# One adaptive-layer and mixture-of-experts kernel: silu ahead of a weight split in tiles 2 to 4, VectorE's tile word read one tile sooner, the fourth expert's weights ahead of the first copies

## The reference

```python
base = jnp.einsum('bsi,oi->bso', x, W_base)
h = jnp.einsum('bsi,ji->bsj', x, Wt)
z = jnp.einsum('bsj,brj->bsr', h, Ab)                    # A[adapter_idx]
l = jnp.einsum('bsr,bor->bso', z, Bb)                    # B_w[adapter_idx]
y = base + jnp.einsum('bso,po->bsp', l, Wp) * sc[:, None, None]
...
probs = jax.nn.softmax(jnp.dot(y, gate_w.T), axis=-1)
topk_w, topk_idx = jax.lax.top_k(probs, TOP_K)           # TOP_K = 2, weights normalised
g = jnp.einsum('th,eih->tei', y, w_gate)                 # INTER = 352
u = jnp.einsum('th,eih->tei', y, w_up)
h = jax.nn.silu(g) * u
expert_out = jnp.einsum('tei,ehi->teh', h, w_down)
out = x + jnp.einsum('te,teh->th', combine, expert_out)
```

## Time and profile before

| what | value |
|---|---|
| median of 3 runs | 355.73 us |
| profiled execution, its own time | 356.19 us |
| its span | 354.3 us |
| PE busy | 337.6 us, 95% of the span |
| DVE busy | 233.0 us, 66% |
| ACT busy | 179.4 us, 51% |
| chain that ended last, PE's share | 76% |
| weights, gate and up: 16 DMAs of 1408 KB | 7.7 us to landing (median) |
| weights, down: 16 DMAs of 768 KB | 9.1 us to landing (median) |
| granted TensorE clock, mean | 0.987 |

### The profile page before, as it was taken

The page is one execution under the profiler, slowest core; times in us unless marked ns, Lnnn a source line. Parts: engine busy times, 40 slices in busy tenths (PEclk is TensorE's granted clock), DMA queues, the critical chain, the costliest instruction groups (busy, mean ns, idle before and its releaser), DMA issues.

```text
span 354.3 us, 7808 instructions
## 1 busy us (share of the span) xinstructions
PE 337.6 (95%) x1879; PEld 298.3 (84%) x1879; DVE 233.0 (66%) x307; ACT 179.4 (51%) x242; POOL 134.1 (38%) x85
## 2 busy tenths in 40 slices
PE   8999999999996998999999999999999999999990
PEld 4777878779886997999899998999989998899970
DVE  0576799986634538485778858788586678778310
ACT  1498622522445463555467554674545476564320
POOL 0000000023527732418374665766645452226231
PEclk9999999999998999999999999999999999999996
DMA  7994865639296899699999995999969789920422
GB/s 277 395 480 134 318 240 177 242 132 335 68 322 137 237 302 310 178 306 281 274 274 303 310 306 160 282 321 266 293 172 285 212 244 293 251 34 4 59 35 37
DMA packets 47352, 82.22 MB, mean 232 GB/s; under 512 B 5488, under 2 KB 22000, under 8 KB 47216
## 3 DMA queue, kind: packets, MB, share of 16 engines
q1 hardware_dynamic: 38336, 62.70, 53.8%
q0 software_dynamic: 8960, 18.89, 23.4%
HBM read 60.59 MB, written 19.92 MB: 227 GB/s over the span
## 4 chain that ended last, share of the span: by engine, by line
PE 76%; DMA 13%; DVE 3%; issue 3%; SPq 2%; ACT 1%; POOLq 1%; DVEq 0%; ACTq 0%
PE bank L690 35%; PE bank L719 19%; DMA xs<-xg 4%; PE bank L546 4%; PE bank L550 4%; PE bank L547 4%; DMA out<-ys,sidx 4%; DMA xg<-y_rows,gidx 3%; PE bank L446 3%; PE bank L664 3%; DMA head_sb<-head 2%; SPq L427 1%; PE bank L477 1%; PE bank L573 1%; DMA y_rows<-y_st 1%
## 5 line engine op out<-in xcount | busy, mean ns | idle before, releaser
L1244 POOL DMA_INDIRECT out<-ys,sidx x40 | 81.4, 2034 | 119.5 <-DMA out<-ys,sidx 56.6
L1223 POOL DMA_INDIRECT xg<-y_rows,gidx x40 | 52.2, 1305 | 94.7 <-issue 79.9
L354 DVE TENSOR_TENSOR w_lo<-w_raw,w_hi (+2 forms) x32 | 76.2, 2383 | 11.9 <-issue 8.1
L690 PE MATMUL bank<-w_hi,xt_hi 128*128 x320 | 82.5, 334 | 0.2 <-issue 0.2
L690 PE MATMUL bank<-w_hi,xt_lo 128*128 x320 | 79.3, 325 | 0.0
L690 PE MATMUL bank<-w_lo,xt_hi 128*128 x320 | 79.3, 324 | 0.0
L352 ACT ACTIVATE w_hi<-w_raw (+2 forms) x32 | 64.6, 2020 | 11.0 <-DMA w_raw<-wall 8.9
L844 ACT ACTIVATE sg<-bank 128x352 f32<-128x352 f32 x40 | 18.5, 462 | 77.0 <-PE bank L690 77.0
L690 PEld LDWEIGHTS bank<-w_lo,xt_hi 128*128 128x128 f32 x320 | 56.4, 190 | 0.0
L690 PEld LDWEIGHTS bank<-w_hi,xt_lo 128*128 128x128 f32 x320 | 56.4, 190 | 0.0
L690 PEld LDWEIGHTS bank<-w_hi,xt_hi 128*128 128x128 f32 x320 | 55.1, 191 | 1.5 <-issue 0.8
(11 more groups left out here) (181 smaller groups left out, 364.7 us busy)
## 6 DMA issues: line engine op xcount, KB each, us to landing
w_raw<-wall SPq DMA_DIRECT2D x16, 1408.0 KB, 7.7
w_raw<-wall SPq DMA_DIRECT2D x16, 768.0 KB, 9.1
xs<-xg SPq DMA_DIRECT2D x128, 64.0 KB
x_st<-xin SPq DMA_DIRECT2D x8, 512.0 KB, 13.0
y_rows<-y_st SPq DMA_DIRECT2D x16, 256.0 KB, 4.0
head_sb<-head SPq DMA_DIRECT2D x2, 640.0 KB, 5.1
wb_sb<-wb SPq DMA_DIRECT2D x2, 512.0 KB, 8.8
wbt_sb<-wbt SPq DMA_DIRECT2D x2, 512.0 KB, 10.7
```

Source lines behind the costliest of these rows:

```text
L354: e.tensor_tensor(w_lo[:, bass.ds(dst, n)], raw, hi, ALU.subtract).then_inc(own, 1)
L690: mm = e.matmul(bank[2 + 2 * s + t % 2][:, 0:INTER], a, w[:, bass.ds(at + (k * GU + s * INTER), INTER)], start=k == 0 and i == 0, stop=k = ...
L1223: e.indirect_dma_start(out=xg[t % NXG][:], out_offset=None, in_=y_dram, in_offset=bass.IndirectOffsetOnAxis(ap=gidx[:, t:t + 1], axis=0)). ...
L1244: e.indirect_dma_start(out=out, out_offset=bass.IndirectOffsetOnAxis(ap=sidx[:, t:t + 1], axis=0), in_=ys[t % NYS][:], in_offset=None, bou ...
```

## The change

ScalarE: in the loop's steps t = 2, 3 and 4 `silu(t)` is put ahead of the gate and up split of tile t+2; from t = 5 on the order stays. VectorE: the word of a tile is read one step sooner, behind `product`, and no longer at the top of the step. SyncE: `later_weights(0)` to `later_weights(3)` all come ahead of `rows_apart(8)`; before, `later_weights(3)`, which loads the weights of the fourth run, came behind it. `later_weights(4)` and all later ones keep their places.

```diff
@@ sync
             e.wait_ge(d_g[N_LATE], 16)
-            for t in range(NTILE + N_COPY):
-                if N_PE <= t < NTILE:
+            for t in range(N_PE - N_COPY + 1):
+                later_weights(t)
+            for t in range(N_PE, NTILE + N_COPY):
+                if t < NTILE:
                     rows_apart(t)
-                if 0 <= t - N_COPY < NTILE - NRAW:
+                if N_PE < t < NTILE - NRAW + N_COPY:
                     later_weights(t - N_COPY)
@@ scalar
-                    if t + 2 < NTILE:
+                    if 5 <= t < NTILE - 2:
                         split_weights(e, count, t + 2, ahead, "gu", a_gu)
                     if t < NTILE:
                         silu(t)
+                    if t < 5:
+                        split_weights(e, count, t + 2, ahead, "gu", a_gu)
@@ vector
+            ahead = tile_word(e, 3)
             with ExitStack() as rest:
                 for t in range(2, NTILE + 1):
                     go_on(e, rest, count, t - 1)
-                    here = word
-                    if t + 1 < NTILE:
-                        word = tile_word(e, t + 1)
+                    here, word = word, ahead
...
                     if t < NTILE:
                         product(t)
+                    if t + 2 < NTILE:
+                        ahead = tile_word(e, t + 2)
                     if N_PE <= t + 2 < NTILE:
                         y_low(t + 2)
```

## The result

| kernel, comparison | median | before beside it | ratio to before, 95% interval |
|---|---|---|---|
| changed | 352.69 us (12 runs) | 355.78 us | 0.9911 [0.9884, 0.9938] |
| changed, second comparison | 351.94 us (6) | 356.56 us | 0.9859 [0.9829, 0.9889] |
| changed, third comparison | 351.65 us (7) | 355.49 us | 0.9910 [0.9877, 0.9943] |

The change makes the kernel 0.9 to 1.4% faster; the medians are 3.1, 4.6 and 3.8 us apart. The ratios and intervals leave out runs over 1.5% above the fastest of their kernel and are not quotients of the medians, which hold all runs. The forecast was 350.8 us, a ratio of 0.986. The sign and the range held, but the forecast gain of 4.99 us is 0.4 to 1.9 us more than came, and two of the three intervals exclude its ratio.

What follows compares the result with a forecast made beforehand. TensorE, full from 140 to 290 us, was taken as the bound, losing time only at waits at tiles 3, 7 and 34. Gains 3.19 + 1.30 + 0.5 = 4.99 us gave 350.8 us, range 349.2 to 353.4.

Steps and rivals of the forecast that it cites:

- The sign and the range: Whole kernel: faster, chance 0.92 for below 353.95 us; range 349.2 to 353.4 us around 350.8.
- Silu ahead of the split: Tile 3: the 3.43 us wait and the clock's fall go; tile 5's transpose comes at 121.62, 3.19 us sooner.
- The new wait: Tile 4's transpose: the old wait returns smaller, 1.81 us, transpose at 114.66; rival that it doesn't form, 348.7 us, chance 0.07.
- Run 3's weights ahead of the copies: Tile 7: copies of tile 9 land by about 125, so the wait goes, 1.30 us; rival of late copies, chance 0.12.
- the gather's delay: Gather ahead of tile 8's copies: delayed at most 3.6 us by run 3's weights, so the copies start at 115.6.
- beside little other traffic: Gather before tile 8's copies: its 4.13 us was without much competing traffic; taking turns could double it, landing at 116.1.
- The word one tile sooner: Tile 34: the read of up to 1.07 us leaves the path; worth 0 to 0.64 us, 0.5 taken.
- 140 to 290 us full as now: TensorE stays busy throughout that stretch, which moves as a whole 4.5 us ahead.
- No new wait came between tiles 8 and 12: Sign against the forecast: it is wrong if a new wait appears between tiles 8 and 12.
- a fall behind 1.81 us: Rival at tile 4: the clock falls after the 1.81 us wait, costing 1.62 us, 352.4 us; chance 0.12.

Runs made afterwards that it cites:

- silu alone: Kernel before with only ScalarE's edit (silu ahead of the split at t = 2 to 4): 356.80 us, ratio 1.0026 [0.9993, 1.0059].
- the word alone: Kernel before with only VectorE's edit (a tile's word read one step sooner): 355.74 us, ratio 0.9999 [0.9980, 1.0019].
- loads alone: Kernel before with only SyncE's edit (fourth run's weight loads ahead of the copies): 355.03 us, ratio 0.9999 [0.9974, 1.0023].
- second profile of before: Kernel before run again, with only masks on two register values added: 356.09 us, ratio 0.9977 [0.9940, 1.0014].
- two gave 2.4 us: Kernel before with ScalarE's and SyncE's edits together, VectorE as before: 352.90 us, ratio 0.9932 [0.9906, 0.9957].
- one number, 4 to 3: Changed kernel with run 2's weight loads released by gather 3 instead of gather 4: 350.43 us, ratio 0.9850; again 350.10 us, ratio 0.9854.
- second profile of the changed kernel: Changed kernel run again without a further edit: 351.94 us, ratio 0.9859 [0.9829, 0.9889].

## Why the prediction was right, and where its sizes were off

**Silu ahead of the split: right in every place.** The wait of 3.43 us and the fall of the clock went. The new wait came at tile 4, and the transpose at 114.66, where the prediction had put it; it costs 1.15 and not 1.81 us, since this execution reached tile 2 0.67 us later (100.00 against 99.33). The transpose of tile 5 came at 121.40 for 121.62. The clock did not fall, in any of the six profiles with this wait (0.86 to 1.70 us in front of the transpose). Up to tile 5's transpose the change gained 3.4 us (means of the profiles: 25.35 us from tile 2's transpose before, 21.94 after). One slip has no effect: the prediction adds 0.57 us from product to transpose on top of the product's 0.51, though the 0.57 runs from the product's start; both sums end before TensorE is free at 106.09. What the prediction missed is the condition. It priced 3.19 us as if nothing behind depended on it; silu alone shows that the gain is lost at tile 6 if run 3's weights land as before.

**Run 3's weights ahead of the copies: the step that failed.** The prediction read 1.30 us of wait at tile 7 in one execution and gave the edit that sum. The wait is in one of the two profiles of before and not in the profiles of the loads or the word alone; the timing of loads alone gives 0. From tile 5 to 8 the changed kernel gained 0.70 us against the mean of the two profiles of before (20.04 to 19.34), nearly all of it against the first. The edit's worth lies elsewhere, at tile 6: silu of tile 6 stands behind the split of tile 8 and so behind run 3's weights. This row of waiting was in the prediction for tile 3, and not applied to the next run. The trace of before had it: the split of tile 8 began at 127.41, when run 3's weights had landed, silu of tile 6 followed at 129.88, and from silu to transpose it takes 1.05 us (108.62 to 109.67), so the transpose could not come before 130.93, where the prediction had it at 128.40. That is 2.5 us of wait with the loads in their old place; silu alone measured 2.71.

The prediction bounded the gather's delay by 3.6 us. The copies came 3.5 us later, but only 2.4 of these are the gather's (6.6 us for 4.13); the other 1.07 is its later issue. The 4.13 us were also not "beside little other traffic": 185 GB/s were moved meanwhile, its own bytes included, against 351 beside run 3's weights. VectorE did wait for copies, against the prediction: 3.62 us for those of tile 8, until 124.17. That cost nothing, and tile 9 was transposed at 127.92, ahead of 129.64, when it was due. The Trainium skill ("DMA: Bandwidth & Descriptors", Queues, rings and completion order) says that a DMA engine takes turns between the rings it has work for. An estimate from it is up to twice 4.13, 8.3 us, beside another queue's load; the measured 6.6 lies between.

**The word one tile sooner: 0.5 forecast, nothing seen.** The split at tile 34 has the short idle time that was foreseen (0.51 us of "issue" where the earlier trace rows has 1.58), and its transpose is on time. Behind it ScalarE is late at the next tile:

```profile
308.64 2.56 ACT L352 ACTIVATE w_hi<-w_raw  x1 [1.08 <-issue]
311.10 0.44 ACT L846 ACTIVATE sg<-bank 128x352 f32<-128x352 f32 x1
```

The 0.64 us of the earlier trace rows was again one execution's; the second profile of before loses 0.10.

**The rest.** "140 to 290 us full as now" failed in two of three profiles of the changed kernel. The split there began 12.6 and 11.3 us after the load's issue. Why the weights took so long is open: nothing was tried at that place, neither the load nor silu's order. That TensorE runs ahead of its loads by more than before (3 us in the first profile) is only the likely reason. No new wait came between tiles 8 and 12.

**The sum.** Two profiles of before and three of the changed kernel, in means, from the table: tile 2 to 8, 45.39 to 41.28, 4.1 gained (4.49 forecast); 8 to 31, 145.06 to 145.75, 0.69 lost (0 forecast); 31 to 39, 50.51 to 50.32, 0.19 gained (0.5 forecast); tile 2's transpose 0.36 later, which no run ties to an edit (it spreads from 99.25 to 100.38 over all fourteen). That makes 3.2 us for 4.99, and the medians say 3.1, 4.6 and 3.8. That the time fell inside the range is in part luck: 3.4 for 3.19 is the mechanism that was forecast, but the 1.30 was read from an execution that lost a close race.

## What to carry to other kernels

- A wait moved out of the way comes back at the next place where the same engine stands in order behind the same kind of landing. Price the gain only up to there: here each edit alone gave nothing, and two gave 2.4 us.
- A wait of about 1 us in one profile may be that execution's alone. Take a second profile of the kernel before ahead of giving it a term; of three waits priced here, only the one at tile 3 (10.2 to 10.8 in every profile where silu and run 2's loads are in their old places) recurred.
- When a split waits for weights, ask first whether the load can be released sooner: one number, 4 to 3, took off about 1.5 us more.

## What the runs showed of the hardware

- The granted clock fell to 0.50 or 0.51 in a stretch of 2 us (the level of 1.2 GHz) behind idle times of TensorE of 2.71 to 3.92 us (six profiles). It fell behind one of 1.80 us too (0.52 in the next stretch), though TensorE had been busy throughout the 4 us ahead of it. It stayed at 1.00 behind one of 1.70 us that had one of 0.61 us ahead of it (second profile of the changed kernel):

```profile
111.45 0.49 PE L722 MATMUL bank<-w_hi,ht_hi 128*128 x1 [0.61 <-DVE ht_lo L1156]
115.50 0.55 PE L667 MATMUL bank<-cs,hh 128*128 128x128 f32 x3 [1.70 <-DVE hh L1165]
```

```profile
116.00:118.00 2.00, 2.00 (x16) 2.00 (x15) 2.00 (x3) 1.08 (x2) 1.76 (x1) 1.00 1.12 284
```

  The forecast had given a fall behind 1.81 us a chance of 0.12; the runs leave that region open. A fall cost 1.5 to 1.75 us (step 4 8.23 to 8.38 against 6.75; step 7 8.04 and 8.05 against 6.30).
- A gather on GpSimd's queue took 4.13 us while 185 GB/s were moved, and 6.6 us while 351 GB/s were, beside run 3's weights (1408 and 768 KB) on SyncE's queue. Each is one gather of one profile.
- TensorE's 23 steps from tile 8 to 31 take 145.02 to 145.10 us in the ten profiles without a wait there, while the load that tile 16's split waits for took 12.6 us from its issue in the first profile of the changed kernel (176.05 to 188.65) and 10.6 in the third (176.41 to 186.97).
